# A twelve-stage decoder on one core: the context half of a depooling stage, and one weight split, moved into earlier stages

## The reference, cut to what matters

```python
# 7: cross attention of x to the given context (8, 256, 512), 8 heads
Q = _split_heads(query, H) * depth ** (-0.5)
k_mem, v_mem = jnp.split(memory, 2, axis=2)
weights = jax.nn.softmax(jnp.einsum('bhqd,bhkd->bhqk', Q, K) + b[0] + -1e+30 * (1.0 - mask), axis=-1)
# 8: gated dense block, int weights, hidden 768
wg, wu, wd = (w.astype(x.dtype) / 127 for w in (w_gate, w_up, w_down))
h = jax.nn.silu(jnp.einsum('bsd,hd->bsh', x, wg)) * jnp.einsum('bsd,hd->bsh', x, wu)
return jnp.einsum('bsh,dh->bsd', h, wd)
# 10: depooling; "h" comes from x, all the rest from the context and from the patch lengths
h = rmsnorm(embeds, g_res)
h = jnp.einsum('bld,ed->ble', h, W_in) + b_in
h_patch = rmsnorm(patch_embeds, g_init)               # context only
boundary_mask = boundary_mask.at[..., jnp.cumsum(patch_lens, axis=1) - 1].set(1)
_, s = jax.lax.associative_scan(comb, (a_b, u), axis=1)   # decaying sum over the patches
plug = jnp.clip(jnp.cumsum(boundary_mask, axis=1) - 1, 0, plen - 1)
return s.reshape(bsz, plen, D_MODEL)[jnp.arange(bsz)[:, None], plug] + h
```

## Time and profile before

| | us |
|---|---|
| median of 3 runs | 2597.81 |
| lowest, highest | 2597.38, 2601.09 |
| the profiled execution's own time | 2597.44 |
| its span in the profile | 2595.6 |
| mean granted TensorE clock | 0.889 of full speed |

### The profile page before, as it was taken

How to read it: one execution, slowest core, us unless ns; L and a number is a source line. 1 busy time by engine, 2 the same in 40 slices (tenths; PEclk the granted TensorE clock), 3 DMA queues, 4 the chain that set the end, 5 groups by cost and what they waited for, 6 DMA issues and landing times.

```text
span 2595.6 us, 34716 instructions
## 1 busy us (share of the span) xinstructions
PE 2041.8 (79%) x12087; PEld 1402.4 (54%) x12087; DVE 1453.6 (56%) x4555; ACT 1093.5 (42%) x2678; POOL 738.9 (28%) x761
## 2 busy tenths in 40 slices
PE   4787786998599996488778898578684979985569
PEld 3444455776455553255445687466462656654436
DVE  5655535544365555378751775797673256665552
ACT  2222231644233331177610555687572346662221
POOL 3111123012122230214237454553144320002123
PEclk9899987999699997799979999789896989996679
DMA  2000001100510001100043555100200020000000
GB/s 93 1 0 33 0 33 54 41 17 1 195 57 1 1 1 63 42 22 21 9 165 110 156 154 194 41 1 1 97 22 25 1 80 1 2 1 35 0 1 33
DMA packets 38828, 117.12 MB, mean 45 GB/s; under 512 B 6640, under 2 KB 24048, under 8 KB 36560
## 3 DMA queue, kind: packets, MB, share of 16 engines
q1 hardware_dynamic: 31024, 93.79, 10.7%
q0 software_dynamic: 7632, 21.11, 2.2%
HBM read 91.68 MB, written 36.04 MB: 49 GB/s over the span
## 4 chain that ended last, share of the span: by engine, by line
PE 59%; DVE 17%; ACT 12%; POOL 7%; issue 3%; DMA 1%; POOLq 1%; SPq 0%; DVEq 0%; ACTq 0%
PE ps L208 36%; PE ps L692 5%; ACT BIG L769 4%; PE ps L664 4%; PE ps L1634 3%; PE ps L711 2%; POOL slots L1883 2%; PE ps L259 2%; ACT BIG L269 2%; PE ps L1646 1%; DVE XN L250 1%; DVE SML L235 1%; POOL SML L214 1%; PE ps L798 1%; PE ps L1173 1%
## 5 line engine op out<-in xcount | busy, mean ns | idle before, releaser
L208 PE MATMUL ps<-BIG 128*128 128x256 f16 (+2 forms) x1632 | 317.9, 352 | 8.9 <-DVE BIG L3054 4.5
L769 ACT ACTIVATE BIG<-BIG,SML 128x256 f32<-128x256 f32 (+1 forms) x768 | 302.5, 483 | 17.3 <-DVE SML L732 17.3
L208 PEld LDWEIGHTS ps<-BIG 128*128 128x128 f16 (+1 forms) x1632 | 217.4, 134 | 98.2 <-issue 60.4
L208 PE MATMUL ps<-XN,BIG 128*128 128x512 f16 x1008 | 235.1, 392 | 22.7 <-DVE BIG L362 17.5
L692 PE MATMUL ps<-CST,BIG 128*128 128x128 f32 x1408 | 213.6, 286 | 38.4 <-ACT BIG L769 22.7
L599 POOL TENSOR_TENSOR BIG<-BIG 128x512 f16<-128x512 f32 x120 | 138.7, 1156 | 336.4 <-ACT BIG L535 278.0
L692 PEld LDWEIGHTS ps<-CST,BIG 128*128 128x128 f32 x1408 | 158.0, 144 | 115.8 <-ACT BIG L769 74.4
L212 POOL TENSOR_SCALAR SML<-SML 128x4 f32<-128x4 f32 (+1 forms) x88 | 21.7, 247 | 696.6 <-DVE SML L981 264.6
L732 DVE CUSTOM_DVE_ANT_0 BIG<-ps,BIG 128x256 f32<-128x256 f32 x512 | 181.3, 420 | 52.1 <-PE ps L664 52.1
L259 PE MATMUL ps<-CST,XN 128*128 128x128 f32 x352 | 72.8, 375 | 156.2 <-DVE XN L250 100.0
L269 ACT ACTIVATE BIG<-ps 128x512 f32<-128x512 f32 (+1 forms) x240 | 126.3, 563 | 138.5 <-PE ps L692 103.0
(11 more groups left out here) (383 smaller groups left out, 4082.2 us busy)
## 6 DMA issues: line engine op xcount, KB each, us to landing
slots<-in_zeros SPq DMA_DIRECT2D x19, 660.0 KB, 22.7
WA<-slots SPq DMA_DIRECT2D x95, 132.0 KB, 2.3
BIG<-in_l1e SPq DMA_DIRECT2D x2, 4224.0 KB, 17.8
BIG<-spread SPq DMA_DIRECT2D x16, 512.0 KB, 6.0
BIG<-in_l0e SPq DMA_DIRECT2D x8, 768.0 KB, 8.8
BIG<-in_ctxT SPq DMA_DIRECT2D x8, 512.0 KB, 3.9
BIG<-in_ctxT SPq DMA_DIRECT2D x16, 256.0 KB, 2.7
BIG<-in_ctx SPq DMA_DIRECT2D x16, 256.0 KB, 3.0
```

Of the source, the lines that this page charges most:

```text
L208: m = T.e.matmul(ps, l, r, start=i == 0, stop=i == len(pairs) - 1)
L769: A.e.activation(s[:, q, 0:kn[q]], s[:, q, 0:kn[q]], ACT.Exp, bias=mx[:, q:q + 1], scale=-1.0).then_inc(*(A.sig("exp", p, n, i) if q else ...
```

## The change

Four things are done.

- **The weights of stage 8 are made ready in stage 7.** POOL's three conversions stand behind the values of the batches 0, 1 and 2 (in place, in WA0). The split's steps are handed to `Aside` as `extra`, one or two steps a quad from quad 6 on, with the two float16 writes cut into pieces of 1024 columns. The halves lie in RING[8192:12032] and WA1.
- **The context part of stage 10 runs beside stage 8.** `patch_pe`, `patch_dve`, `patch_act`, `patch_pool` are generators of which one step is taken after each of the 24 units. The squares of the context go from ACT to DVE (L2190 of the new file). The one-hot rows and the ones that they are multiplied with become float16, so that "hits" is two float16 matmuls. The small preparation (`patch_ends_*`) stands ahead of stage 8's first unit.
- **What stays in stage 10** (`embed_*`) is ordered by a new table `ORDER_10` with a row for each engine, each digit one step of that group. The bias is added on POOL, not DVE.
- **Loads:** the context is loaded in stage 7 behind the loads of batch 4, the decay table at the start of stage 8.

```diff
+ORDER_10 = {
+    "pe": "0100110232123323",
+    "dve": "01021030010110210321122323323233",
+    "act": "0123010230112233",
+    "pool": "010122330123",
+}
...
+            def beside(self, n):
+                if n >= 6:
+                    next(self.extra, None)
+
             def begin(self, n):
+                self.beside(n)
...
             def ended(self, n):
+                self.beside(n)
...
+                if c["p"] == 7 and b == 4 and 8 in phases and 10 in phases:
+                    load_context()
...
+                if p == 7 and 8 in phases and b < 3:
+                    dequant(b)
...
         def dense_pe(c, tailed=True, background=None):
...
-            finish(split_pe(RD, p, c["r"], 3 if c["bias"] is not None else 2))
+            if p != 8 or 7 not in phases:
+                finish(split_pe(RD, p, c["r"], 3 if c["bias"] is not None else 2))
+            background = background and background(RD)
...
         def l2_ffn_pe(c):
-            dense_pe(c)
+            if 10 in phases:
+                patch_ends_pe(S10, Banks(marks, (4,)))
+            dense_pe(c, background=(lambda ring: patch_pe(S10, ring)) if 10 in phases else None)
...
+        def patch_pe(c, ring):
+            for k in range(B + 3):
+                if 0 <= k - 1 < B:
+                    b, before = ring.take(("hits", k - 1), ("cn", k - 1))
+                    waits(T, *before)
+                    waits(T, ("oh", k - 1))
+                    group(PS[b][:, 0:256], [(c["ones"], c["OH"][(k - 1) % 2][:, h, :]) for h in range(2)]).then_inc(
+                        *T.sig("hits", k - 1))
+                yield
+                if 0 <= k - 2 < B:
+                    d = k - 2
+                    b, before = ring.take(("dep", d), ("depc", d))
+                    waits(T, *before)
+                    waits(T, ("cxn", d), ("decay",))
...
+        def patch_dve(c):
...
+                    for t in range(2 * b, 2 * b + 2):
+                        V.e.tensor_tensor_reduce(out=c["junk"], in0=CX[:, t, :], in1=CX[:, t, :], scale=1.0, scalar=0.0,
+                                                 op0=ALU.mult, op1=ALU.add, accum_out=c["ss2"][:, t:t + 1]).then_inc(
...
+        def embed_pool(c, g):
+            x = X[:, 4 * g:4 * g + 4, :]
+            waits(G, ("w10",))
+            G.e.tensor_tensor(x, x, rows(W[10]["bin"], 4), ALU.add).then_inc(*G.sig("xin", g))
+            yield
+            waits(G, ("ss1", g))
+            pow_half(c["r1"][:, 4 * g:4 * g + 4], c["ss1"][:, 4 * g:4 * g + 4], 1.0 / 256, 1e-5, "r1", g)
```

More of the change, by code:

```diff
@@ L230, in weights, with ordered @@
                 SP.e.dma_start(dst.bitcast(I32) if p == 8 else dst, a[f"w{p}"]).then_inc(*SP.sig(f"w{p}", by=16))
+        def ordered(q, table, units):
+            for x in table[q.tag]:
+                next(units[int(x, 36)], None)
+            finish(*units)
         def norm_stats(p, g, *after):
@@ L601, in units_pool @@
                         c += 1
+                        if background is not None:
+                            next(background, None)
                 if tail is not None:
@@ new lines, in patch_act, with patch_pool @@
+        def patch_act(c):
+            for k in range(B + 3):
+                if 0 <= k - 3 < B:
+                    b = k - 3
+                    waits(A, ("dep", b))
+                    A.e.activation(c["CX"][:, 2 * b:2 * b + 2, 256:512], bank("dep", b).rearrange("p (h d) -> p h d", h=2),
+                                   ACT.Copy).then_inc(*A.sig("depc", b))
+                yield
+                yield
+        def patch_pool(c):
+            for k in range(B):
+                yield
+                waits(G, ("ss2", k))
+                pow_half(c["r2"][:, 2 * k:2 * k + 2], c["ss2"][:, 2 * k:2 * k + 2], 1.0 / 512, 1e-5, "r2", k)
+                yield
@@ new lines, in embed_pe @@
+        def embed_pe(c, g):
+            R, CX, win = c["ring"], c["CX"], part("win", 10)
+            waits(T, ("w10",), ("res", g))
+            turn_tiles(R, "rt", XN, 10, g)
+            yield
+            for d in range(2 * g, 2 * g + 2):
+                b, before = R.take(("xp", d), ("xb", 10, d))
+                waits(T, *before)
+                waits(T, ("sel", d), ("depc", d), ("rt", 10, g, 0), ("rt", 10, g, 1))
+                for h in range(2):
+                    m = group(PS[b][:, h * 256:(h + 1) * 256],
+                              [(CX[:, 2 * d + i, tok(h)], CX[:, 2 * d + i, 256:512]) for i in range(2)]
+                              + [(XT[:, k, tok(2 * d + h)], win[:, k, :]) for k in range(2)])
+                m.then_inc(*T.sig("xp", d))
+                yield
+            if after(10) is not None:
+                norm_turn(R, after(10), g)
@@ new lines, in embed_act @@
+        def embed_act(c, g):
+            for i in range(4 * g, 4 * g + 4):
+                A.e.activation(c["sq"][i % 2], XN[:, i, :], ACT.Square, accum_out=c["ss1"][:, i:i + 1]).then_inc(
+                    *(A.sig("ss1", g) if i % 4 == 3 else A.step()))
+                if i % 2:
+                    A.wait_ge(*A.last())
+            yield
+            norm_copy(A, 10, g, 0, "rt")
+            yield
+            if after(10) is not None:
+                norm_copy(A, after(10), g, 0)
+                yield
+                norm_upper(after(10), g)
@@ L2251, in combined @@
                 yield from ()
-        def ordered(q, group, batch):
-            live = {}
-            for x in ORDER_6[q.tag]:
-                i = int(x, 16)
-                if i not in live:
-                    live[i] = group(i) if i < NG else batch(i - NG)
-                next(live[i], None)
-            finish(*live.values())
         def levels_dve(key, src, nb, kind, small, *after_):
```

318 lines of the change are left out of this document (163 added, 155 removed).

## The result

The changed kernel takes 2539.03 us, median of 4 runs (2537.97 to 2541.62), against 2598.65 for the kernel before beside it (4 runs, 2597.38 to 2601.09): a ratio of 0.9771, with a 95% interval of 0.9754 to 0.9788. The prediction said 2542.0, in a range from 2518 to 2570. The profiled execution of the changed kernel is its longest run, 2541.62 us, with a span of 2539.8.

What follows compares the result with a forecast made beforehand. The prediction saw serial chains between engines in stage 10 and stage 8's start, with stage 8 then bound by PE. 2597.4 - 76.8 (stage 10) + 13.5 (stage 8) + 8.0 (stage 7) = 2542.1 us, range 2518 to 2570.

Steps and rivals of the forecast that it cites:

- Stage 10, 62 predicted: Stage 10 was to fall from 138.8 to about 62 us, a gain of 76.8, with bounds 57 and 92.
- The walk: Stage 10's remaining work on x summed from row durations in written order: start, eight products, end; 60 us, plus 2.
- Stage 8's start, 21.2 predicted: Before stage 8's first unit, 23.3 us of conversion and split go and 2.1 of preparation come: gain 21.2.
- PE's own work: Stage 8: added matmuls for "dep" (14.5 us) and float16 "hits" (1.7) lengthen PE's work by 16.2 us.
- PE's waits: Stage 8: PE waits for DVE, blocked beside POOL, and once for the hits' bank: +17 us, bounds 6 and 26.
- The clock: Stage 8: PE's pauses of up to 5 us make some matmuls run at 1.2 GHz, costing 1.5 us.
- Stage 7, 8.0 predicted: Stage 7: inserted split work costs its length less small slack on DVE and ACT: +8.0 us, bounds 2 and 16.4.
- The load of the context: Rival in stage 7: the context's load makes batch 5's keys or mask late, +10 us, 2552; chance 0.08.
- Blocking is not felt: Rival: POOL and DVE fall into step; stage 8's waits are 6, stage 10 is 59, total 2526; chance 0.15.
- Stage 10 at 1.2 GHz throughout: Rival: PE's pauses keep the clock down, stage 10 takes 92 us, total 2572; 0.13 for both long stage 10 versions.
- the parts in a chain: Rival: stage 10's groups don't overlap, 96 us instead of 62, total 2576; 0.13 for both long stage 10 versions.
- a slow stage 8: Rival, slower than before: pauses keep stage 8 at 1.2 GHz throughout, +94 us, total 2636; chance 0.04.

Runs made afterwards that it cites:

- the second execution: The changed kernel itself, unaltered, measured and profiled again: 2540.38 us, ratio 0.9770 to the kernel before.
- the short additions: Against the changed kernel, POOL writes only 8 of 512 columns of each lower half of stage 8's hidden values: 2533.02 us, ratio 0.9747.
- the scalings: Stage 10, against the changed kernel: POOL's roots before its additions, 2567.99 us (ratio 0.9767); with additions also after DVE's scaling, plus two stage 8 edits, 2522.70 us (0.9705).
- the first two together: Changed kernel with hits read first and squares on ACT in stage 8, plus POOL's roots first in stage 10: 2555.53 us on a slower chip, ratio 0.9722.

## Why the prediction was right, point by point

**Stage 10, 62 predicted, 57.7 and 59.4 measured.** The walk was start 15.2, middle 33.9, end 10.8; measured are 13.6, 33.0 and 11.1. The products come every 3.46 us, where the walk took 3.62; the blocking at the start was 3.7 us (eight scalings in 5.35 instead of 3.34, the next four in 3.36 instead of 1.67), where I took 3.4. It is 0.3 us below the 58 to 66 that I named. The 2 us for the 1.2 GHz start were paid in the second execution and not in the first.

**Stage 8's start, 21.2 predicted.** 20.9 by the profiles, 21.0 by the run with the split put back.

**PE's own work, 16.2 predicted, 16.7 measured.**

**PE's waits, 17 predicted, 9.7 measured: the term that was mis-sized.** Its form was right in half. DVE is the bound by its blocked instructions, and the bank of the hits brings one wait at the seventh pair; it was 4.4 us where I said 5. But I let PE wait for DVE's product when DVE is late, and all three long waits (1.2, 3.9 and 4.4 us) are for the bank of the hits; with the hits read first 6.7 us of them were gone though DVE was busy as long. In size two factors were wrong. I let DVE be late in eight pairs by 2.3 us each, less 6; but DVE was the bound only from 1998.7 to 2030.3, four pairs. And the blocking was 1.2 to 1.6 us a pair, less than the 2.3: a square beside one of POOL's roots kept its 0.69 us, and a part of each addition falls beside DVE's products, which stay at 730 to 753 ns in all 88 of them. At one point blocking went further than I said. I counted only instructions with two inputs from SBUF; but L2197 and L2222, with one full input, took up to 1.12 and 1.22 us instead of 0.35, and L2209 up to 1.07 instead of 0.29. The Trainium skill has this, under "SBUF — State Buffer", section "Who interferes with whom": where their operands allow it, tensor_scalar, copy and cast can run in a mode that takes the port pair shared with GpSimd. By that rule they belonged into the sum; the trace agrees by these lengths, but which mode they ran in no run here shows.

**The clock, 1.5 predicted, about 5 measured.** I priced the pauses by their number and not by what follows: PE's busy time is 117.93 us where the same work took 112.78 without the waits. Waits and clock together were 18.5 predicted and 14.9 measured, so the two errors partly cancel.

**Stage 7, 8.0 predicted, 9.9 measured.** The reductions were right (3.3 against 3.0 to 3.6). What is short is the rest, 4.7 against 6.3 to 6.9; which of the tiny operations, the pieces and POOL's conversions it is, was not tried apart. The load of the context costs nothing, as said.

**The rivals.** "Blocking is not felt" is refuted by the short additions (-9.6 us in stage 8) and by the scalings (7.62 against 3.45 us). Stage 10 at 1.2 GHz throughout, the parts in a chain, and a slow stage 8 did not come. And 5 us of the agreement between the sum and the profiled execution are chance, as said above.

## What to carry to other kernels

A wait on the engine that sets the pace can cost more than its length: 6.7 us of waits went with 5.2 more of lost clock here, though only with 1.1 in the kernel with the split put back. Before work is moved from a busy engine, look in which order it reads what others wait for: one reading moved up by a few instructions took 11.9 us off the main stretch, as much as 15 us of work taken away from DVE (11.2) and more than 27 us taken from POOL (9.6), and the first two together gave little more than one (14.2). When an engine starts earlier, look at what it now runs beside: POOL's roots first gave nothing until its additions also kept out of the scalings' way.
